# Attention on one core: halves of a pair of heads, with scores and maxima by turns and the value products behind them

## The reference, cut to what matters

```python
Q = jnp.einsum('btd,hkd->bthk', x, W_Q) + b_Q      # K, V likewise
scores = jnp.einsum('bqhk,bshk->bhqs', Q, K) / jnp.sqrt(d_head)
attn = jax.nn.softmax(scores, axis=-1)
out_h = jnp.einsum('bhqs,bshk->bqhk', attn, V)
return jnp.einsum('bqhk,hdk->bqd', out_h, W_O) + b_O
```

## Time and profile before

| | us |
|---|---|
| median of 3 runs | 1192.4 |
| lowest, highest | 1190.06, 1194.43 |
| profiled execution, its span | 1192.9 |
| PE busy | 1129.3 (95%) |
| DVE busy | 816.6 (68%) |
| POOL busy | 759.8 (64%) |
| ACT busy | 600.7 (50%) |

### The profile page before, as it was taken

The page is one execution under the profiler, slowest core; times in us unless marked ns, Lnnn a source line. Parts: engine busy times, 40 slices in busy tenths (PEclk is TensorE's granted clock), DMA queues, the critical chain, the costliest instruction groups (busy, mean ns, idle before and its releaser), DMA issues.

```text
span 1192.9 us, 19525 instructions
## 1 busy us (share of the span) xinstructions
PE 1129.3 (95%) x7549; PEld 660.4 (55%) x7549; DVE 816.6 (68%) x1208; ACT 600.7 (50%) x867; POOL 759.8 (64%) x393
## 2 busy tenths in 40 slices
PE   5899999999999999999999999988888998989998
PEld 1445555555555555555555555776644444445786
DVE  5575666655755656655666754723798999998887
ACT  3434345344343444444444344544886664956753
POOL 3477778777777768767678973023089887896100
PEclk9899999999999999999999999998999999999999
DMA  6000000000000000000000204357464544341000
GB/s 199 1 1 2 1 1 1 2 1 1 2 1 2 1 2 1 2 2 1 1 1 11 68 30 147 111 148 223 147 219 135 167 142 158 127 159 54 10 9 18
DMA packets 38076, 68.85 MB, mean 58 GB/s; under 512 B 5952, under 2 KB 24128, under 8 KB 37984
## 3 DMA queue, kind: packets, MB, share of 16 engines
q1 hardware_dynamic: 34976, 64.52, 17.1%
q0 software_dynamic: 1024, 2.10, 0.5%
q10 hardware_dynamic: 1984, 0.98, 0.3%
HBM read 61.30 MB, written 6.16 MB: 57 GB/s over the span
## 4 chain that ended last, share of the span: by engine, by line
PE 78%; issue 7%; DVE 6%; POOL 5%; ACT 2%; DMA 2%; SPq 0%; POOLq 0%; DVEq 0%; ACTq 0%
PE psum L594 20%; PE psum L563 16%; PE psum L580 6%; PE psum L610 6%; PE psum L567 5%; PE psum L974 3%; PE psum L672 3%; PE psum L880 3%; PE psum L957 3%; POOL hc L2101 3%; PE psum L625 2%; PE psum L645 2%; PE psum L749 2%; PE psum L738 1%; DVE psum L1781 1%
## 5 line engine op out<-in xcount | busy, mean ns | idle before, releaser
L2013 POOL TENSOR_TENSOR psums<-psums,prob 128x1024 f32<-128x1024 f32 x180 | 426.9, 2372 | 106.4 <-ACT prob L1065 84.3
L1494 DVE TENSOR_REDUCE mx<-psum 128x2 f32<-128x1024 f32 x256 | 301.8, 1218 | 214.2 <-PE psum L580 214.2
L1065 ACT ACTIVATE prob<-psum 128x1024 f32<-128x1024 f32 x256 | 243.4, 1025 | 218.2 <-PE psum L567 218.2
L594 PE MATMUL psum<-prob,V 128*64 128x512 f32 x1024 | 258.4, 604 | 0.0
L2101 POOL TENSOR_TENSOR hc<-hs,cc 128x1024 f32<-128x1024 f32 x64 | 151.5, 2368 | 21.5 <-DVE hs L1788 19.0
L1788 DVE TENSOR_TENSOR_SCAN hs<-dA,psum 128x1024 f32<-128x1024 f32 x64 | 146.3, 2287 | 2.2
L880 PE MATMUL psum<-hc,ident 128*128 128x512 f32 x256 | 123.6, 606 | 2.5 <-DVE slot_rows_h L1796 1.4
L594 PEld LDWEIGHTS psum<-prob,V 128*64 128x64 f32 x1024 | 62.0, 136 | 98.3 <-issue 92.6
L2013 POOL TENSOR_TENSOR psums<-prob 128x1024 f32<-128x1024 f32 x30 | 71.4, 2382 | 63.4 <-ACT prob L1065 63.4
L563 PE MATMUL psum<-q_hi,k_hi 64*128 64x512 f32 x512 | 108.4, 419 | 0.0
L567 PE MATMUL psum<-guard,row_one 64*128 64x512 f32 x512 | 101.6, 393 | 2.2 <-DMA guard<-mrow 2.2
(11 more groups left out here) (290 smaller groups left out, 1686.9 us busy)
## 6 DMA issues: line engine op xcount, KB each, us to landing
cc<-C_rows SPq DMA_DIRECT2D x64, 512.0 KB, 3.7
kq_wts<-in_e_rows SPq DMA_DIRECT2D x14, 578.0 KB, 4.7
e_wts<-in_e_rows SPq DMA_DIRECT2D x10, 578.0 KB, 4.1
e_w<-in_e_rows SPq DMA_DIRECT2D x6, 578.0 KB, 4.3
slots_in<-e_zero SPq DMA_DIRECT2D x2, 960.0 KB, 8.2
slots_out<-e_y SPq DMA_DIRECT2D x30, 64.0 KB, 3.0
x<-in_x SPq DMA_DIRECT2D x2, 512.0 KB, 5.0
e_w<-in_e_w SPq DMA_DIRECT2D x1, 1024.0 KB, 7.8
```

Of the source, the lines that this page charges most:

```text
L594: ins = pe.matmul(A.O[HALF[s], :], A.V[pair % 2][:, j, s * DH:(s + 1) * DH], A.prob[unit(pair, c, j) % NPB][:, s * CH:(s + 1) * CH], start ...
L1065: act.activation(A.prob[n % NPB][:, :], slots.bank("score", pair, c, j).rearrange("p s n -> p (s n)"), ACT.Exp, scale=float(DH) ** -0.5).t ...
L1494: dve.tensor_reduce(K.A.mx[:, :, t, c], slots.bank("max", pair, t, c), AXX, ALU.max).then_inc(*slots.inc("max", pair, t, c))
L2013: pool.tensor_tensor(total[:, :], (K.A.prob[(n - 1) % NPB] if j == 1 else total)[:, :], K.A.prob[n % NPB][:, :], ALU.add).then_inc(*K.psum ...
```

## The change

A pair before the last is now two phases, one for each query half c. A phase is eight times (maximum, score), then the output projection of the pair before, then eight value products with the projections, the values, the row and the sum in between. Parts:

- The order list: 8 maxima (of the next pair) and 8 scores by turns; all 16 maxima are those of the next pair. The steps of `EARLY` go behind the sixth value product, or behind `take` at the end.
- The slots are given by name (`slot_of`): maximum j has slot 2j mod 3 and score j has slot (2j+1) mod 3. That is the same as taking turns, so that each step has the slot of the step three places ahead of it.
- `sum` becomes `sumhalf` for all pairs: each query half is summed alone, half 0 in phase 1 of its own pair, half 1 in phase 0 of the next pair.
- Ten `prob` buffers instead of seven; `psums` and `oraw` once instead of twice.
- The last pair keeps its four phases.

```diff
-NPB = 7
+NPB = 10
...
+def phase(pair, c):
+    last, nxt, ahead = pair - 1, pair + 1, pair + 2
+    maxes = [(nxt, *m) for m in MAXES[NT * c:NT * (c + 1)]]
+    chunks = [chunk for chunk in CHUNKS[2 * c:2 * c + 2] if ahead < PAIRS and (ahead, *chunk) not in STAGED]
+    first, second = ([*map(lambda chunk: project(ahead, chunk), chunks)] + [[], []])[:2]
+    pv = [("pv", pair, c, j) for j in range(NT)]
+    early = [EARLY.get((pair, 2 * c + i), []) for i in range(2)]
+    order = []
+    for j in range(NT):
+        order += largest(maxes[j]) + [("score", pair, c, j)]
+    if c == NC - 1:
+        order.append(("cols", nxt))
+    if last >= 0:
+        order.append(("out", last, c))
+    order += first[:1] + pv[:1] + first[1:] + pv[1:3] + second[:1] + pv[3:4] + second[1:] + pv[4:5]
+    if c == NC - 1:
+        order += [("row", nxt), ("rowed", nxt)] + pv[5:6] + [("values", nxt, 1), ("valued", nxt, 1)] + early[0] + pv[6:7] + [("sumhalf", pair, 0)]
     else:
...
+        order += [("values", nxt, 0), ("valued", nxt, 0)] + pv[5:6] + early[0] + pv[6:7] + [("sumhalf", last, NC - 1)] * (last >= 0)
+    return order + pv[7:] + [("take", pair, c)] + early[1]
+def slot_of(step):
+    kind, pair, *k = step
+    if kind == "max" and pair:
+        return 2 * k[0] % 3
+    if kind == "score" and pair < LAST:
+        return (2 * k[1] + 1) % 3
+    if kind == "out" and pair < LAST - 1:
+        return 1
...
 def act_take(K, act, pair, c):
     A = K.A
     act.wait_ge(*K.pv_done.at(pair, c, NT - 1))
-    if pair > 1:
-        act.wait_ge(*K.slots.full.at("out", pair - 2, c))
-    act.copy(A.oraw[pair % 2][:, c * CH:(c + 1) * CH], A.O).then_inc(*K.taken.inc(pair, c))
+    if pair:
+        act.wait_ge(*K.slots.full.at("out", pair - 1, c))
+    act.copy(A.oraw[:, c * CH:(c + 1) * CH], A.O).then_inc(*K.taken.inc(pair, c))
```

More of the change, by code:

```diff
@@ L190, in largest @@
     return [step for m in maxes for step in (("max", *m), ("maxed", *m))]
[L193 to L201, removed]
-    else:
[L203 to L231, removed]
@@ L234, in last_phase @@
+def slot_of(step):
[6 more added lines that the diff above has]
+        return 1
+    if kind == "score":
+        return (2 + k[1]) % 3 if k[0] == 0 else k[1] % 3
+    if kind == "out":
+        return (2, 0)[k[0]] if pair == LAST else 1 + k[0]
 def last_phase(f):
@@ L241, in last_phase @@
     pv = [("pv", pair, c, j) for j in js]
-    order += pv[:2] + second + pv[2:3] + [("sum", pair - 1)] * (f == 0) + pv[3:]
+    order += pv[:2] + second + pv[2:3] + [("sumhalf", pair - 1, NC - 1)] * (f == 0) + pv[3:]
     if f % 2:
@@ L422, in rows_of, with plan_slot @@
     return K.act_rows if n in ACT_ROWS else K.ln_rows
+def plan_slot(K, by, step, bank, now=True):
+    slots, work = K.slots, K.work
+    slots.plan(by, *step, bank=bank, now=now)
 def plan_all(K):
@@ L431, in plan_all @@
     work.take_turns(7)
-    K.slots.n = 1
     for step in K.order:
@@ L453, in plan_all @@
         elif kind == "score":
-            K.slots.plan("act", *step)
+            plan_slot(K, "act", step, slot_of(step))
             if k[2]:
@@ L457, in plan_all @@
         elif kind == "max":
-            K.slots.plan("dve", *step, bank=1 + len(K.slots.place) % 2 if k[0] == 0 else None, now=False)
+            plan_slot(K, "dve", step, slot_of(step) if k[0] else 1 + len(K.slots.place) % 2, now=False)
         elif kind == "maxed":
@@ L461, in plan_all @@
         elif kind == "out":
-            K.slots.plan("dve", *step)
-        elif kind in ("sum", "sumhalf", "gdir"):
+            plan_slot(K, "dve", step, slot_of(step))
+        elif kind in ("sumhalf", "gdir"):
             work.plan("dve", *step)
@@ L527, in added, with wait_slot @@
     return (K.psum_late if pair == LAST else K.psum_done).at(pair, c, j)
-def sums(pair, c):
-    return ("sumhalf", pair, c) if pair == LAST else ("sum", pair)
+def wait_slot(K, pe, step):
+    slots = K.slots
+    if slots.place[step][1] == ("first",):
+        pe.wait_ge(*K.work.empty("proj", 1, "q", 1))
+    if slots.free(*step):
+        pe.wait_ge(*slots.free(*step))
 def pe_turn_norm(K, pe, n, g):
@@ L555, in pe_score @@
         pe.wait_ge(*low_part(K, pair, "q", c))
[L556 to L560, removed]
+    wait_slot(K, pe, ("score", pair, c, j))
     for part, (left, right) in enumerate(((A.k_hi[r], A.q_hi[r]), (A.k_hi[r], A.q_lo[r]), (A.k_lo[r], A.q_hi[r]))):
@@ L633, in pe_row @@
     pe.transpose(K.work.bank("row", pair)[:, 0:P], K.A.nmx[:, :], K.ident[:, :]).then_inc(*K.work.full.inc("row", pair))
[L636 to L647, removed]
 def pe_sum_half(K, pe, pair, c):
@@ L668, in pe_out @@
     pe.wait_ge(*K.taken.at(pair, c))
-    pe.wait_ge(*slots.free("out", pair, c))
+    wait_slot(K, pe, ("out", pair, c))
     for t in range(4):
         for s in range(2):
-            ins = pe.matmul(both[:, s, t * P:(t + 1) * P], A.oraw[pair % 2][HALF[s], (4 * c + t) * P:(4 * c + t + 1) * P],
+            ins = pe.matmul(both[:, s, t * P:(t + 1) * P], A.oraw[HALF[s], (4 * c + t) * P:(4 * c + t + 1) * P],
                             A.wo[HALF[s], p * D:(p + 1) * D], start=True, stop=True)
@@ L1546, in dve_out @@
     tiles = [pair // NPAIR * NT + 4 * c + t for t in range(4)]
-    dve.wait_ge(*K.work.empty(*sums(pair, c)))
+    dve.wait_ge(*K.work.empty("sumhalf", pair, c))
     dve.wait_ge(*slots.full.at("out", pair, c))
@@ L1682, in dve_late_sums @@
         return
-    total = A.psums[pair % 2][c]
+    total = A.psums[c]
     dve.wait_ge(*K.slots.empty("score", pair, c, j))
     if j == 1:
-        dve.wait_ge(*K.work.full.at("sum", pair - 2))
+        dve.wait_ge(*K.work.full.at("sumhalf", pair - 1, c))
     else:
@@ L2006, in pool_score @@
         return
-    n, total = unit(pair, c, j), K.A.psums[pair % 2][c]
+    n, total = unit(pair, c, j), K.A.psums[c]
     pool.wait_ge(*K.slots.empty("score", pair, c, j))
-    if j == 1 and pair > 1:
-        pool.wait_ge(*K.work.full.at("sum", pair - 2))
+    if j == 1 and pair:
+        pool.wait_ge(*K.work.full.at("sumhalf", pair - 1, c))
     if K.psum_done.given:
```

29 lines of the change are left out of this document (13 added, 16 removed).

## The result

The changed kernel takes 1224.28 us (median of 4 runs, 1222.5 to 1227.47) beside 1191.99 us for the kernel before: ratio 1.028, 95% interval 1.0255 to 1.0306. It is 2.8% slower. The profiled executions have spans of 1221.8 us and 1192.9 us.

What follows compares the result with a forecast made beforehand. PE's own queue was taken to bound the attention. To 1192.9 us came 21 for the order and 8 for EARLY, giving 1222 for the profiled execution and 1221 for the median; range 1189 to 1239 us.

Steps and rivals of the forecast that it cites:

- What bounds the kernel: In the attention PE's own queue sets the time, busy 44.82 of 44.90 us in one pair; other engines have slack.
- the terms of the sum: PE's step times, changes of number format and output waits in one pair before the change: 44.8 us against 44.9 measured.
- The gain: Order of steps in a pair: six fewer round trips save 1.8 us, the output projection's waits 0.4; 2.2 in all.
- round trip: On PE, changing number format between fp32 and fp32r and back: 0.3 us each, eight a pair before, two after.
- The wait of the output projection: Before the change, the output projection waits for DVE to empty its slot: 0.2 us, twice a pair.
- The cost, the closed chain: First half of a phase: DVE's chain over three slots takes 2.73 us for two turns, stalling PE 3.6 a pair.
- Balance: Stall less gain from the new order: +1.4 us a pair, +21 us over 15 pairs.
- The second half: Value products, projections and the rest of a phase: some 11.8 us without waits; second projection covered by 0.4, guard about 2.5.
- The buffers: The ten buffers of probabilities wait for nothing, so they add nil.
- EARLY: Layer norms in pairs 3 and 9 delay PE 2.7 us each; with half clock and small DVE work, +8 us.
- The clock as a rival: PE's clock falls once a pair because of the stalls: 40 us more, 1262 us; chance 0.04.
- The sum: Whole kernel: 1192.9 + 21 + 8 = 1222 us for the profiled execution, 1221 for the median.

Runs made afterwards that it cites:

- x3: Changed kernel with each maximum's reduction over 256 of 512 keys and each exponential over the first head alone: 1174.5 us, ratio 0.9821 to the kernel before.
- v2: Kernel before with the output projection behind the third value product of its phase instead of ahead of it: 1189.5 us, ratio 0.9977.
- x5: Kernel before with each phase's second value product moved between the second and third of the three maxima: 1207.41 us, ratio 1.0101.
- x2: Changed kernel with each reduction to a maximum over the first 256 of 512 keys alone: 1203.37 us, ratio 1.0057 to the kernel before.
- v4: x1 with a fourth slot, banks 6 and 7, while scores and maxima run: 1169.62 us, ratio 0.9815 to the kernel before.
- x6: Changed kernel with seven buffers of probabilities instead of ten: 1258.28 us, ratio 1.0529 to the kernel before.
- x1: Changed kernel with layer norm rows of pairs 3 and 9 moved behind the second phase's sixth value product: 1215.69 us, ratio 1.0169 to the kernel before.
- v1: Half-pair phases reordered against the changed kernel: eight scores in a row, six maxima among value products, layer norms as in x1: 1201.14 us, ratio 1.0042 to the kernel before.

## Why the prediction was right, step by step

- **What bounds the kernel, and the terms of the sum.** Right. The sum of the terms without any stall gave 42.7 us a pair; x3, which has the changed order and no chain, shows 42.5.
- **The gain, 2.2 us a pair.** Near in sum (45.07 before, 42.5 in x3: 2.5), wrong in its reason, and near partly by luck. What a round trip costs is not the change of number format but that of the weights' form (x3, v2, x5). A trip costs 0.35 us instead of 0.3, and eight are saved instead of six, since the two output projections had one each. The wait of the output projection was half of what I took (v2). At these prices the gain would be some 3.0 (an estimate); where the last 0.5 goes is not shown.
- **The cost, the closed chain.** Right in place and size. Two turns took 2.75, 2.74 and 2.87 us against 2.73, score 1 went at 1.82 as forecast, and the eight turns were over at 11.2 against 11.0. x2, x3 and v4 show that it is this chain: shortening DVE's link moves the limit to ACT's, shortening both or adding a slot removes it, with PE's instructions unchanged. Stall by x3 against the changed kernel: 46.4 - 42.5 = 3.9 us a pair, against my 3.6.
- **Balance.** +1.35 us a pair against +1.4, 20 us against 21.
- **The second half.** 11.72 us in one phase and 12.27 in the other, which has the row, against 11.8 for both; the row's own time and its changes of form were not in the 11.8. There was no wait of PE for the guard or bank 7. That the cover was thin (0.4 us) is what x6 showed.
- **The buffers.** That ten wait for nothing was right. That fewer would do was right for eight and wrong for seven.
- **EARLY.** Place and mechanism right, size short: ACT's rows ended 5.5 us into the phase instead of 4.4, the two waits were 3.4 us instead of 2.7, and the clock fell behind both, not at one time in two. The two cost 11.6 us, where I had 7.6. The small DVE work, for which I had 1, cost 1.2 at pair 12. x1 gives 13 back.
- **The clock as a rival.** The rule of the Trainium skill ("TensorE: Matmul & The Clock Gate", "A second HAM failure mode: psum-queue depth-cycling") would have had the clock go up and down with the waits at every slot. The trace does not agree for this kernel: from 60 to 200 us, where PE's loads wait for DVE's slots in every phase (11.2 us in all, 36 times), the granted clock is 1.00 throughout. From 60 to 740 us it fell only behind the two waits of 3.4 us and behind the small matmuls in pair 11.
- **The sum.** For the profiled execution 1222 was forecast and 1221.8 measured. That this is so close is partly luck. EARLY was about 5 too small, pairs 10, 11, 13 and 14 had 3.7 more that I had not counted, and against these stand the first pair with 5.4 less and 2.4 at the two ends, which I had not counted either. The median is 1224.3 against 1221. The 3 us between are no term of the sum: I took the median to lie 0.5 below the span of the profiled execution, as before, and here it lies 2.5 above it.

## What to carry to other kernels

Where two engines empty the slots that a third fills in turns, matching rates are not enough. Add up the chain once round (emptying, release, refill, start of the next emptying) and divide it by the steps it spans; if that is more than the filler's own work, try one more slot. Here it was worth more than the other order that was tried (v4 against v1), and memory that is idle in just this stretch was that slot. And before a wait is called harmless, look at what stands behind it in its own engine's queue, not only at who needs its result.

A second one is for reading: under a PE that was busy for 98% of these 11.2 us, nearly a fifth of the time was stall, since pipelined matmuls are recorded longer than their distance. Starts of like steps, and the waits of the weight loads, show it. And when two things change at the same place (here number format and form of the weights), look in the trace for a place where only one of them does.

## What the runs showed of the hardware that I had not expected

- A change of the weights' form, from 128 rows by 64 columns to 64 by 128 and back, costs about 0.35 us (x5). From fp32r to fp32 with the form kept costs nothing that shows (score 7 to `out` in x3: 0.92, as between scores).
- A step that has waited for its slot pays about 0.1 us more for the weights, which are otherwise loaded under the matmul before (first matmul 0.50 instead of 0.39, the next 0.33 behind it instead of 0.23).
- Short waits for slots, in every phase from 60 to 200 us of the changed kernel, left the granted clock at 1.00. After each of the two waits of 3.4 us it was at its half level for 3.4 or 6.8 us, the length differing between two like events of one execution. It also fell once in x5 (240.5, 3.4 us) with no wait ahead, behind 64 matmuls of one column, and not behind the other sums of that stretch.
